# A decoder layer on one core: the output projection as float32r upper and lower products, its weights and rows divided on ScalarE and VectorE

## What is computed

```
# x: 16 sequences of 128 rows, D = 256; H = 8 heads of 128
u = layernorm(x)
q, k = l2norm(u @ Wq), l2norm(u @ Wk);  v = u @ Wv;  alpha = sigmoid(u @ Wg)
S_t = alpha_t * S_(t-1) + k_t v_t^T;  o_t = q_t S_t            # per head
x = x + concat_heads(o) @ Wo                                   # the output projection
# cross attention with ctx: softmax(layernorm(x) (ctx W^T)^T) ctx
x = x + cross(layernorm(x), ctx, W)
# two of eight experts for each sequence, gelu between down and up
x = x + experts(layernorm(x))
```

## Time and profile before

| | |
|---|---|
| median of 3 runs | 547.12 us (544.78 to 547.32) |
| the profiled execution | 546.16 us |
| its span, first to last instruction | 544.4 us, mean granted clock 0.956 |
| TensorE busy | 483.6 us, 89% of the span |
| VectorE busy | 380.4 us, 70% |
| ScalarE busy | 355.6 us, 65% |
| transfers | 20.35 MB, mean 37 GB/s |

### The profile page before, as it was taken

One profiled execution on the slowest core, in us unless ns is written; L12 is line 12 of the kernel. 1 busy time (PEld: TensorE's weight loads), 2 busy tenths in 40 slices (PEclk: granted clock), 3 DMA queues, 4 the chain that ended last, 5 costly groups with the idle time before them and its releaser, 6 DMA issues. The chain is left out here.

```text
span 544.4 us, 25975 instructions
## 1 busy us (share of the span) xinstructions
PE 483.6 (89%) x11232; PEld 399.9 (73%) x11232; DVE 380.4 (70%) x1069; ACT 355.6 (65%) x826; POOL 96.9 (18%) x102
## 2 busy tenths in 40 slices
PE   1899999999989899999988999999989999775416
PEld 1587788778878788788876888888878888564315
DVE  5778977766795988766786987857786987514531
ACT  4778776766767667687767677686769576432111
POOL 1221211111122121320122211421110213201120
PEclk9999999999989999999999999999999999886756
DMA  8900000001010100120110100221000100200021
GB/s 324 279 4 4 4 4 4 4 3 42 4 43 2 42 4 4 42 81 9 36 42 4 41 4 4 61 62 41 4 4 4 41 4 24 59 20 20 0 77 39
DMA packets 15264, 20.35 MB, mean 37 GB/s; under 512 B 1200, under 2 KB 12976, under 8 KB 15152
## 3 DMA queue, kind: packets, MB, share of 16 engines
q1 hardware_dynamic: 13872, 14.49, 8.0%
q0 software_dynamic: 1280, 4.20, 2.8%
HBM read 16.60 MB, written 2.10 MB: 34 GB/s over the span
## 5 line engine op out<-in xcount | busy, mean ns | idle before, releaser
L450 ACT COPY states<-states 128x512 f32<-128x512 f32 (+1 forms) x160 | 94.6, 591 | 91.0 <-DVE states L661 84.5
L661 DVE TENSOR_TENSOR states<-states,spans 128x512 f32<-128x512 f32 x128 | 88.5, 691 | 15.0 <-ACT states L450 4.2
L364 POOL TENSOR_TENSOR rnorm<-norm_sq,neg_half 128x4 f32<-128x4 f32 x32 | 33.0, 1032 | 289.4 <-DVE norm_sq L704 289.4
L1147 PE MATMUL acc<-wo_sb,oT_sb 128*128 128x256 f32 x256 | 62.0, 386 | 0.7 <-ACT oT_sb L477 0.7
L1062 PE MATMUL ring<-wv_sb,xnT 128*128 128x256 f32 x384 | 54.5, 290 | 1.0 <-DVE wv_sb L895 1.0
L1049 PE MATMUL ring<-xnT,wk_sb 128*128 128x512 f32 x192 | 53.6, 415 | 1.7 <-DVE xnT L767 1.6
L1049 PE MATMUL ring<-xnT,wq_sb 128*128 128x512 f32 x192 | 53.4, 413 | 0.1
L1147 PEld LDWEIGHTS acc<-wo_sb,oT_sb 128*128 128x128 f32 x256 | 47.4, 195 | 6.2 <-ACT oT_sb L477 0.9
L692 DVE COPY_PREDICATED blocks<-owned,lo_bank 128x128 f32<-128x128 uint32 x128 | 38.5, 301 | 18.4 <-PE lo_bank L1072 15.0
L1049 PE MATMUL ring<-xnT,wg_sb 128*128 128x512 f32 x192 | 50.2, 396 | 0.3 <-DVE wg_sb L895 0.3
L1062 PEld LDWEIGHTS ring<-wv_sb,xnT 128*128 128x128 f32 x384 | 48.0, 188 | 1.5 <-DVE wv_sb L895 1.1
(11 more groups left out here) (147 smaller groups left out, 879.8 us busy)
## 6 DMA issues: line engine op xcount, KB each, us to landing
x_buf<-x_dram SPq DMA_DIRECT2D x4, 512.0 KB, 4.1
ctxT_sb<-ctxT_dram SPq DMA_DIRECT2D x8, 256.0 KB, 3.6
ctx_sb<-ctx_dram SPq DMA_DIRECT2D x4, 512.0 KB, 4.6
out_dram<-x_mid SPq DMA_DIRECT2D x8, 256.0 KB, 2.2
states<-wk_dram SPq DMA_DIRECT2D x1, 1024.0 KB, 5.9
states<-wg_dram SPq DMA_DIRECT2D x1, 1024.0 KB, 8.0
states<-wq_dram SPq DMA_DIRECT2D x1, 1024.0 KB, 10.0
v_sb<-wv_dram SPq DMA_DIRECT2D x1, 1024.0 KB, 12.1
```

The source lines that it names most:

```text
L364: nc.gpsimd.tensor_tensor(rnorm[:, m % 4, GB:2 * GB], norm_sq[:, GB:2 * GB], neg_half[:, GB:2 * GB], ALU.pow).then_inc(rk_set, 1)
L450: nc.scalar.copy(dst, src).then_inc(carry_set, 1)
L661: nc.vector.tensor_tensor(dst, src, by, ALU.mult).then_inc(decayed, 1)
L1147: last = mm(accs[z][:, D * m:D * m + D], oT_sb[:, n % 2, T * b:T * b + T], wo_sb[:, h], start=(h == 0 and m == 0), stop=(h == H - 1 and m ...
```

## The change

`wo_sb` becomes an upper and a lower part in float32r. `wo` is loaded into `sel`, which is free at that time (`stage_o`). In the first eight units ScalarE rounds one head of it at the end of the unit (`wo_upper`, 128 x 256), and VectorE makes the rest of it in the next unit (`wo_lower`). `oT_sb` has no second buffer any more: its two places are upper and lower. ScalarE's `oT_out` writes the upper one, and VectorE subtracts it from the PSUM tile (`oT_lower`, 128 x 512), in the unit between `q_decayed` and the tail part "late". The output projection waits for that, and its 4 matmuls become 12. To make room for the larger `wo_sb`, `ctxT_sb` becomes a view of `ctx_sb`, with the loads of the two in turn, and `downT` a view of `xn`, so that the layer norm at h = 2 waits for the "hid" product of unit h = 0 instead of a transpose of the group before.

```diff
-        wo_sb = sb("wo_sb", [P, H, D])
+        wo_sb = sb("wo_sb", [P, 2, H, D], F32R)
-        ctxT_sb = sb("ctxT_sb", [P, KC, GB, T])
+        ctxT_sb = ctx_sb[:].rearrange("p (c b) (h t) -> p c (b h) t", c=KC, t=T)
-        oT_sb = sb("oT_sb", [P, 2, N])
+        oT_sb = sb("oT_sb", [P, 2, N], F32R)
-        downT = sb("downT", [P, GB, KC, P])
+        downT = xn[:].rearrange("p b (c n) -> p b c n", c=KC)
+        stage_o = view(sel, 0, [[1, H * D]])
...
-                        "o": (o_set, n + 1), "oT": (oT_set, n + 1)}[kind]
+                        "o": (o_set, n + 1), "oT": (oT_lo_set, n + 1)}[kind]
...
-            load_ctx(0)
             for i in range(1, NG):
                 sp.wait_ge(tail_mm, TAIL["keys", i - 1, 1])
-                load_ctxT(i)
+                load_ctx(i - 1)
...
                 sp.wait_ge(tail_mm, TAIL["cross", i - 1, 1])
-                load_ctx(i)
+                load_ctxT(i)
+            sp.wait_ge(tail_mm, TAIL["keys", NG - 1, 1])
+            load_ctx(NG - 1)
...
-                nc.scalar.copy(oT_sb[:, n % 2], ring_of(("oT", n))[:]).then_inc(oT_set, 1)
+                nc.scalar.copy(oT_sb[:, HI], ring_of(("oT", n))[:]).then_inc(oT_set, 1)
+            def wo_upper(h):
+                act.wait_ge(wo_in, 16)
+                nc.scalar.copy(wo_sb[:, HI, h], stage_o[:, D * h:D * h + D]).then_inc(wo_hi, 1)
...
+                if n < H:
+                    wo_upper(n)
                 tail_part(n, "end")
...
+            def oT_lower(n):
+                dve.wait_ge(oT_set, n + 1)
+                nc.vector.tensor_tensor(oT_sb[:, LO], ring_of(("oT", n))[:], oT_sb[:, HI].bitcast(F32),
+                                        ALU.subtract).then_inc(oT_lo_set, 1)
+            def wo_lower(h):
+                dve.wait_ge(wo_hi, h + 1)
+                nc.vector.tensor_tensor(wo_sb[:, LO, h], stage_o[:, D * h:D * h + D], wo_sb[:, HI, h].bitcast(F32),
+                                        ALU.subtract).then_inc(wo_split, 1)
...
-                        ln_normalize(("mid", t), x_mid, ("x3T", t - 1, 1) if t > 0 else ("xT", 1, 1))
+                        ln_normalize(("mid", t), x_mid, ("hid", t - 1, 0) if t > 0 else ("xT", 1, 1))
...
+                if 1 <= n <= H:
+                    wo_lower(n - 1)
+                if n >= 2:
+                    oT_lower(n - 2)
                 tail_part(n, "late")
...
+            oT_lower(U - 2)
             o_scaled(U - 1)
             tail_part(U, "end")
+            oT_lower(U - 1)
...
-                pe.wait_ge(oT_set, n + 1)
+                pe.wait_ge(oT_lo_set, n + 1)
+                if i == 0:
+                    pe.wait_ge(wo_split, h + 1)
...
-                    last = mm(accs[z][:, D * m:D * m + D], oT_sb[:, n % 2, T * b:T * b + T], wo_sb[:, h],
-                              start=(h == 0 and m == 0), stop=(h == H - 1 and m == 1))
+                    for part, (a, w) in enumerate(PARTS):
+                        last = mm(accs[z][:, D * m:D * m + D], oT_sb[:, a, T * b:T * b + T], wo_sb[:, w, h],
+                                  start=(h == 0 and m == 0 and part == 0), stop=(h == H - 1 and m == 1 and part == 2))
```

More of the change, by code:

```diff
@@ L131, in decoder_kernel, with view @@
         sel = sb("sel", [P, GB, 2 * D + 1])
-        downT = sb("downT", [P, GB, KC, P])
+        downT = xn[:].rearrange("p b (c n) -> p b c n", c=KC)
+        def view(tensor, start, dims):
+            whole = tensor[:]
+            return bass.AP(whole.tensor, whole.offset + start, [list(whole.ap[0])] + dims)
         stage_k, stage_g, stage_q = (
@@ L155, in decoder_kernel @@
                              "attnT_set", "oT_set"))
-        q0_set, decayed, span_set, kept, norm_sq_set, v_set, o_set = (
-            sem(n) for n in ("q0_set", "decayed", "span_set", "kept", "norm_sq_set", "v_set", "o_set"))
+        q0_set, decayed, span_set, kept, norm_sq_set, v_set, o_set, oT_lo_set = (
+            sem(n) for n in ("q0_set", "decayed", "span_set", "kept", "norm_sq_set", "v_set", "o_set", "oT_lo_set"))
+        wo_in, wo_hi, wo_split = sem("wo_in"), sem("wo_hi"), sem("wo_split")
         rk_set, rq_set, ln_stat, ln_var, ln_rstd, ln_out = (
@@ L261, in positive @@
                 engine.wait_ge(s, value)
-        def view(tensor, start, dims):
-            whole = tensor[:]
-            return bass.AP(whole.tensor, whole.offset + start, [list(whole.ap[0])] + dims)
         def state_at(n, l):
@@ L285, in span_at @@
             return 0 if l < 2 else 2 * (N // 2 - N // 2 ** l)
-        N_W, N_C = 16 * 4, 16 * 2
+        N_W, N_C = 16 * 3, 16 * 2
         block = stack.enter_context(nc.Block())
@@ L318, in _ @@
                 sp.dma_start(dst[:], src).then_inc(c_in, 16)
-            sp.dma_start(wo_sb[:], wo.rearrange("(h p) n -> p h n", p=P)).then_inc(w_in, 16)
+            sp.dma_start(stage_o.rearrange("p (h n) -> p h n", h=H), wo.rearrange("(h p) n -> p h n", p=P)).then_inc(wo_in, 16)
             load_x(1)
@@ L500, in downT_out @@
                 for z in range(2):
-                    tail_to(downT[:, 2 * z:2 * z + 2].rearrange("p b c n -> p (b c n)"), ("downT", t, z), downT_set)
+                    tail_to(xn[:, 2 * z:2 * z + 2].rearrange("p b n -> p (b n)"), ("downT", t, z), downT_set)
             def gelu(t):
```

2 lines of the change are left out of this document (removed).

## The result

The changed kernel takes 566.21 us (median of 4 runs, 565.54 to 567.16) against 546.35 us for the kernel before on the same chip: a ratio of 1.037 with an interval of 1.033 to 1.040, some 20 us slower. The forecast was 552.0 us with a range of 544.0 to 557.0. Its direction is right, its size is 14 us short. The profiled execution took 565.54 us with a span of 563.7 us (before 546.16 and 544.4), and the mean granted clock is 0.938 for 0.956.

A forecast was written before the change was run, and what follows sets the result against it. TensorE's stream was taken to bound most units. From 546.2 us, delays of 1.9 + 1.9 + 2.6 + 1.0 less 4.6 gained (2.8), plus 3.0 for the clock, gave 552.0 us, range 544.0 to 557.0.

The forecast's parts named there:

- What bounds the kernel: Whole kernel: TensorE's stream, busy 89%, bounds most units; its large wait is for VectorE's layer norm, six times, 9.2 us.
- In units 14 and 22 the unit behind is full and nothing waits: Units 14 and 22: the added subtraction makes nothing wait, so no cost was put there.
- The gain: Output projection: float32r saves 0.19 us a head, 1.54 us for 1.73, counted in 24 heads: 4.6 us gained.
- three for four: Output projection, rival: three passes replace four and save 0.43 us a head, 10.4 us; 543.2 us in all, chance 0.03.
- h = 2 and 3: Layer norm units: the subtraction delays xn by 0.63 us at h = 2 and 0.95 us at h = 3, 1.9 us each in sum.
- The first three units: Start-up: dividing wo and subtracting for oT delay the transposes of unit 3 by 2.6 us, low end 1.0, high end 3.2.
- The clock: Longer waits for xn: two more falls to half clock at 1.5 us each, 3.0 us; none to all five, 0 to 7.5.
- the clock falls at every long wait: Rival: falls at all long waits, also at the start and unit 31, cost 7.5 us; 556.5 us in all, chance 0.13.
- Units 29 to 31: Units 30 and 31: the choice of experts starts later, behind the subtraction, and TensorE waits in unit 31: 1.0 us.
- The end: End chain: the last product is 0.65 us later, but the residual waits for x_mid's store: nothing, high end 0.5 us.
- shared tiles: Loads of ctx and ctxT in turn, and downT in xn: no cost.
- up to 0.63 us in some 20 units: Plain units: the subtraction's cost if VectorE's 1.60 us of idle time were gone, 12 us; taken as nothing.

The follow-up runs named there:

- the shared tiles alone: Kernel before with only ctxT_sb as a view of ctx_sb, downT as a view of xn and the loads in turn: 547.67 us, ratio 1.0005.
- the product alone: Changed kernel without VectorE's subtraction of oT, 549.70 us; in a second kernel also without its eight subtractions for the weights, 548.44 us.
- spare products: Extra matmuls, sums overwritten, ahead of xn's transposes at h = 2 and 3: nine in the changed kernel, 565.53 us; five in the kernel before, 550.64 us.

## Why the prediction was wrong

**What bounds the kernel.** It read TensorE's list of waits and looked for trouble only where TensorE already waited for VectorE. That found the units h = 2 and 3 and nothing else. A unit in which TensorE does not wait can still be paced by VectorE to within a few tenths: ahead of k in unit 15 the kernel before has 0.7 us between the end of `v_scaled` (230.41) and k (231.11), as its own timeline shows:

```profile
229.73 0.68 DVE L713 TENSOR_TENSOR v_sb<-ring,rnorm 128x512 f32<-128x512 f32 x1
231.66 0.42 DVE L678 TENSOR_TENSOR spans<-alpha 128x256 f32<-128x256 f32 x1 [1.24 <-ACT alpha L415]
```

```profile
231.11 1.18 PE L1049 MATMUL ring<-xnT,wk_sb 128*128 128x512 f32 x4
```

**"In units 14 and 22 the unit behind is full and nothing waits": this step failed**, and it is the largest error, 6.1 us measured in units 12 to 15, 20 to 23 and 28 against -1.8. That the next unit has work for TensorE is no cover, because that work needs banks of the ring, which the delayed queue frees. The prediction saw that chain in the start-up, where it named the bank of v for k and the handing over between ScalarE and VectorE, and did not follow it from unit 12 to 15 and from 20 to 23. The run with the subtraction in all but h = 2 and 3 shows it: 10.1 us, in units to which the sum gave 1.0 us beside the start-up. In its trace units 12 to 15 are 3.5 us and units 20 to 23 are 3.1 us longer than with the shared tiles alone, without a half-clock stretch in them.

**The gain** was too small per head and counted in too many heads. The prediction took v's 1.54 us and 0.19 us a head; measured are 1.56 us for 1.83 where block products follow, and the plain units are 0.34 us shorter on average. The row of v that it used has another successor than the projection, and the difference of 0.19 us came out too small by a third. But it counted 24 heads, and in the main only ten units kept it, 3.4 us for 4.6. In the two kernels with the product alone even that is given back elsewhere. The Trainium skill ("FP8 and Floating Point Precision", "TensorE Precision Notes") gives true FP32 4 passes. The prediction's estimate from it, three for four, was 0.43 us a head; the measured gain, 0.27 us, lies between this and the row of v.

**h = 2 and 3.** The mechanism was right, and the waits for xn grew to 15.0 us as forecast. The sum, 3.8 us and 3.0 us for the clock, less 0.8 for four projections, is 6.0 us, and 7.2 were measured. The run with the subtraction at h = 2 and 3 alone has 0.5 to 0.7 us more in each h = 2 unit, the forecast's 0.63. At h = 3 it took 0.95, and unit 19 has 0.96 without the clock.

**The first three units**: 2.6 us forecast, 3.6 measured. k of unit 2 waits 1.03 us for v's bank where 1.15 was forecast, and the transposes of unit 3 start at 73.16 us; less the 3.4 us by which unit 1 starts later (24.72 + 9.13 to 26.52 + 10.68), that is 2.3 us later than 67.46. The rest of unit 3 is its half-clock stretch, which the sum had under the clock. The 1.8 us ahead of v of unit 0 were in no term.

**The clock.** Two more falls at 1.5 us were taken; there are three more, and they cost 1.1 us each in the pair of profiles with and without spare products. 3.0 and 3.3 us: right in sum by luck, one fall too few and each too dear. The whole time puts all four at 2 us only, so the 3.3 is an upper estimate. The rival "the clock falls at every long wait" would have been nearer in the total, but for a reason that is not the true one.

**Units 29 to 31**: 1.0 us forecast, 5.3 measured, 3.5 of it in unit 31, where how much is the clock is not separated. The choice of experts starts at 476.57 behind the subtraction, as described, and TensorE then waits 1.44 us for o_sb in unit 31, beside the wait for the blocks that was there before. And g of unit 29 waits for the bank of o, at h = 5:

```profile
455.01 1.67 PE L1075 MATMUL ring<-xnT,wg_sb 128*128 128x512 f32 x6 [1.28 <-DVE o_sb L738]
```

**The end** and the **shared tiles** cost nothing, as forecast. The end is 2.8 us shorter, with the clock at half in other stretches of it.

**The chances.** Slower had 0.62, which was right. The range failed because all of its cases shared the step that nothing waits outside of h = 2, 3, the start and unit 31. The prediction had the price in hand: up to 0.63 us in some 20 units, 12 us, if the idle time were gone. It was dismissed from one plain unit with 1.60 us of idle time, and the ten plain units are indeed free of it; the 18 units with a tail are not plain.

## What to carry to other kernels

Before an instruction is added to a queue, find for each kind of unit the next idle time behind it that is longer than the instruction and ends with an engine that does not itself wait for this queue (a wait for ScalarE was no cover here, since ScalarE waited for VectorE's decays; a wait for TensorE's lo_bank was). Everything between, up to that point, is late by its length, and what is not absorbed adds to the next one, and each release of a PSUM bank among it must be compared with the moment at which the next user of the bank wants it. A list of waits shows who waits now, not who has only 0.7 us left. A mean of 70% busy said nothing here: five sixths of what was added came out in the whole time.

## What the runs showed of the hardware

A 128 x 512 subtraction takes VectorE 684 ns from SBUF alone and 690 ns with one operand in PSUM, 6 ns more. A head's product of 256 columns is 1.56 us to the next start with three float32r products (12 matmuls) and 1.83 us as one in float32 (4). A stretch at 1.2 GHz behind a wait of TensorE costs 1.3 to 1.8 us in its own unit (the pairs with and without spare products), but at h = 2 only 0.7 us with the next unit, whose transposes wait for VectorE anyway (units 10 and 11, 35.43 us with the stretch and 34.75 or 34.76 without). And the first transfer of 1 MB, wk, with the same loads issued ahead of it, landed after 5.9 to 8.2 us, for a cause that stays open.
